# First attention of a decoder kernel: queries projected with features on the partitions, for two batches at a time

## The chip, the cores and the metric

The kernel runs on one core of a Trainium2 chip. The core has a matrix engine (TensorE), three engines for vectors (VectorE, ScalarE, GpSimd), a queue that issues DMAs (SyncE, SP in the rows), an on-chip memory of 128 partitions (SBUF) and eight accumulation banks of 128 x 512 fp32 (PSUM), which GpSimd cannot reach in this kernel. The metric is the device time of one execution in microseconds (us), lower is better; the time of before is the median of three.

## The reference

Two decoder layers over x of 4 batches x 256 tokens x 256 features, each of attention, an adjacency or bilinear step with a side input, and a feed-forward step. The change concerns the first attention alone: 32 heads, queries from a low rank of 192, keys and values from a latent of 64 and a shared rotary part of 64.

```python
q = rms_norm(hidden_states @ q_a_w, q_a_ln_w) @ q_b_w
q = q.reshape(B, S, NH, DQK)
q_pass, q_rot = (q[..., :DN], q[..., DN:])
ckv = hidden_states @ kv_a_w
c_kv, k_rot = (ckv[..., :KVLR], ckv[..., KVLR:])
kv = rms_norm(c_kv, kv_a_ln_w) @ kv_b_w
...
q_rot = apply_rope(q_rot, pos)      # x1*cos - x2*sin, x1*sin + x2*cos on halves of 32
k_rot = apply_rope(k_rot[:, :, None, :], pos)[:, :, 0, :]
scores = (einsum('bqhd,bkhd->bhqk', q_pass, k_pass) + einsum('bqhd,bkd->bhqk', q_rot, k_rot)) * scale
scores = jnp.where(causal[None, None], scores, jnp.finfo(scores.dtype).min)
p = jax.nn.softmax(scores, axis=-1)
out = jnp.einsum('bhqk,bkhd->bqhd', p, v).reshape(B, S, NH * DV)
return out @ o_w
```

Beside it, independent of it and needed right after it, stands an adjacency per batch: similarities of the side input, of which the top 76 of 256 in each row are kept, through a sigmoid, and mixed with the normalised attention output.

## The kernel before, in words

The key part of kv_b is absorbed into the query's weights, so that every head has a query of 128 features for each token: 64 latent ones and 64 rotary ones. All heads share the keys of a batch (`keyT`, features on the partitions), and the values are the latent part of `key_tok`. The 32 heads are worked in 8 groups `g` of 4. Products of projections are made of fp32 numbers split in a high and a low part, three products for each; a query bank is five products of 512 columns.

For each batch `b` and group `g` the steps are: `q` (TensorE: two banks, one for each tile of 128 tokens, tokens on the partitions, 4 heads x 128 features in the columns; VectorE: three multiplications into `rope_buf`; ScalarE: latent part to `q_tok`; GpSimd: adds the two rotary products into `q_tok`), `qT` (TensorE: 8 transposes of 128 x 128 back into the same banks; ScalarE: two copies to `qT`), twice `s` (scores of two heads; VectorE masks and takes the row extremes in two pieces, 256 and 128 wide, since the causal half is left out; ScalarE: exp), `norm` (VectorE reciprocal, GpSimd multiplies), `pT` (transposes of probabilities), then `pv`, `out`. A group's weights come by DMA into one of two raw buffers and are split into high and low parts (`w_q`, `w_v`).

The adjacency's steps are `adj_sim` (TensorE), ten rounds `adj_top` on VectorE (MAX of 8, MATCH_REPLACE), two masks `adj_mask` on VectorE and `adj_T`; batch `b` starts after the masks of `b - 1`. Behind the attention of a batch stand statistics, normalisation and mixing (`att_stats`, `att_mix`, `mix_norm`), and then the router and the experts.

What sets the order is a planner, which runs when the program is built: every step has parts with an engine and a cost, needs, and places that it holds (banks, `probs`, `qT`, `rope`, `q_tok`). It takes the step that can start soonest on an engine, among near ones the one with the longest way to the end, and writes an order for each engine. Each engine then executes its own list strictly in that order, and waits on semaphores. A change of steps or costs thus moves instructions on all engines. `mm` is line 1011 (every product), `transpose` 1025, ScalarE's `copy` 1389, VectorE's `tt` 1680, GpSimd's `tt` 2136.

## Time and profile before

| | |
|---|---|
| median of three runs | 800.99 us (800.61 to 803.52) |
| the profiled execution | 801.79 us |
| its span in the trace | 799.9 us, 15236 instructions |
| mean granted TensorE clock | 0.976 |
| busy: TensorE, its weight loads, VectorE, ScalarE, GpSimd | 751.4 (94%), 636.4 (80%), 566.4 (71%), 506.4 (63%), 354.6 (44%) us |
| chain that ended last | TensorE 85%, VectorE 11% |

Engines in the rows: PE is TensorE, PEld its weight loads, DVE VectorE, ACT ScalarE, POOL GpSimd, SPq the queue of SyncE. Busy shares are averages over stages with different bounds; which engine sets the time in a stage is read from the chain of waits there. A product's listed duration overlaps the next one, so its price in a dense row is the distance between starts. fp32 products that aren't split by hand appear as two instructions each.

### The profile page before, as it was taken

Reading aid. Unit: us, or ns where it says so; the run is one execution under the profiler, and the core shown is the slowest. Engines: PE = TensorE matmul, PEld = TensorE weight load, DVE = VectorE, ACT = ScalarE, POOL = GpSimd, SP = SyncE. Lnnn points to the kernel's source line nnn. Section 1 sums busy time; section 2 is a strip of 40 time slices with the busy share of each in tenths; the row PEclk is TensorE's granted clock in tenths of the full one; section 3 lists DMA queues with packets and bytes.
Section 4 is the critical chain, followed back from the end, with each engine's and each line's share of the span. In section 5 each row is a group of like instructions: output and inputs, shape, how many; then the busy total and the mean of one; then the engine's idle time right before and its main releaser. Section 6 shows DMA issues by size and latency. Waiting matters only on the chain.

```text
span 799.9 us, 15236 instructions
## 1 busy us (share of the span) xinstructions
PE 751.4 (94%) x5060; PEld 636.4 (80%) x5060; DVE 566.4 (71%) x1909; ACT 506.4 (63%) x1321; POOL 354.6 (44%) x595
## 2 busy tenths in 40 slices
PE   6899999999999999999987999999879999969995
PEld 4578888888888888888765887888768888748884
DVE  2879889888679854656897756546787575656844
ACT  2669683878558774786654646676457757626541
POOL 1436441554236441566662445544752122347640
PEclk9899999999999999999997999999999999979998
DMA  8700002200040001100020021111110001000320
GB/s 274 208 3 2 2 2 74 74 1 2 1 146 2 2 1 40 41 2 1 1 80 0 1 77 38 45 40 40 40 42 3 2 3 31 13 2 0 119 66 27
DMA packets 27479, 30.95 MB, mean 39 GB/s; under 512 B 4412, under 2 KB 24518, under 8 KB 27400
## 3 DMA queue, kind: packets, MB, share of 16 engines
q1 hardware_dynamic: 27400, 29.96, 12.1%
q8 instruction: 41, 0.67, 0.4%
q14 instruction: 38, 0.31, 0.1%
HBM read 28.77 MB, written 1.05 MB: 37 GB/s over the span
## 4 chain that ended last, share of the span: by engine, by line
PE 85%; DVE 11%; issue 1%; POOL 1%; DMA 1%; ACT 1%; SPq 0%; DVEq 0%; ACTq 0%
PE bank L1011 73%; PE bank L1025 12%; DVE x L1677 1%; DVE y L1683 1%; POOL probs L2133 1%; DVE bn L1711 1%; DMA xT_plain<-in_xT 1%; DVE probs L1828 1%; DVE top_tok L2044 1%; DVE rope_tmp L1680 1%; DVE g_pair_lo L1680 0%; DVE key_tok L1683 0%; DVE u_pair_lo L1680 0%; DVE stat L1683 0%; DVE router_buf L1683 0%
## 5 line engine op out<-in xcount | busy, mean ns | idle before, releaser
L2133 POOL TENSOR_SCALAR probs<-probs,soft 128x256 f32<-128x256 f32 (+1 forms) x256 | 104.9, 431 | 76.2 <-DVE soft L1836 75.9
L1475 ACT ACTIVATE probs<-probs,soft 128x256 f32<-128x256 f32 (+1 forms) x256 | 113.0, 447 | 2.0 <-DVE soft L1828 2.0
L2136 POOL TENSOR_TENSOR w_split_lo<-w_raw,w_split_hi 128x512 fp32r<-128x512 f32 (+2 forms) x57 | 74.3, 1312 | 65.3 <-ACT w_split_hi L1389 65.2
L2136 POOL TENSOR_TENSOR q_tok<-rope_buf 128x256 f32<-128x256 f32 x64 | 47.7, 748 | 106.1 <-DVE rope_buf L1680 105.9
L1011 PE MATMUL bank<-keyT,qT 128*128 128x256 f32 (+1 forms) x512 | 92.3, 328 | 0.0
L1011 PEld LDWEIGHTS bank<-keyT,qT 128*128 128x128 f32 x512 | 82.9, 190 | 9.4 <-issue 0.3
L1828 DVE CUSTOM_DVE_ANT_0 probs<-bank,mask 128x256 f32<-128x256 f32 (+1 forms) x256 | 78.5, 354 | 9.4 <-PE bank L1011 9.0
L1680 DVE TENSOR_TENSOR rope_buf<-bank,rope 128x128 f32<-128x128 f32 (+1 forms) x192 | 52.0, 328 | 32.6 <-PE bank L1011 32.2
L1389 ACT ACTIVATE qT<-bank 128x512 f32<-128x512 f32 (+1 forms) x96 | 53.6, 592 | 23.3 <-PE bank L1025 22.8
L1011 PE MATMUL bank<-w_split_hi,xT_hi 128*128 128x512 f32 (+1 forms) x160 | 64.8, 405 | 2.1 <-DVE xT_lo L1683 1.6
L1389 ACT ACTIVATE probsT<-bank 128x384 f32<-128x384 f32 x128 | 54.0, 489 | 13.4 <-PE bank L1025 13.3
L1011 PE MATMUL bank<-w_split_hi,xT_lo 128*128 128x512 f32 (+1 forms) x160 | 61.9, 387 | 0.0
L2136 POOL TENSOR_TENSOR probs<-probs 128x512 f32<-128x512 f32 x32 | 41.6, 1309 | 39.2 <-ACT probs L1558 38.1
L1011 PE MATMUL bank<-w_split_hi,g_pair_hi 128*128 128x256 f32 x192 | 54.6, 284 | 2.7 <-issue 1.5
L1011 PE MATMUL bank<-w_split_lo,g_pair_hi 128*128 128x256 f32 x192 | 54.0, 281 | 0.0
L1011 PE MATMUL bank<-w_split_hi,g_pair_lo 128*128 128x256 f32 x192 | 54.0, 281 | 0.0
L1389 ACT ACTIVATE q_tok<-bank 128x256 f32<-128x256 f32 x64 | 24.2, 385 | 46.6 <-DVE rope_buf L1680 46.2
L1011 PE MATMUL bank<-xT_hi,w_split_hi 128*128 128x512 f32 x128 | 52.1, 407 | 0.0
L1025 PE MATMUL bank<-identity,probs 128*128 128x128 f32 x384 | 50.7, 274 | 1.1 <-POOL probs L2133 1.0
L1011 PE MATMUL bank<-xT_hi,w_split_lo 128*128 128x512 f32 x128 | 51.4, 401 | 0.0
L1011 PE MATMUL bank<-xT_lo,w_split_hi 128*128 128x512 f32 x128 | 51.3, 401 | 0.0
L2044 DVE TENSOR_REDUCE top_tok<-bank 128x2 f32<-128x512 f32 x64 | 40.3, 686 | 14.2 <-PE bank L1011 13.8
(227 smaller groups left out, 2077.1 us busy)
## 6 DMA issues: line engine op xcount, KB each, us to landing
w_raw<-in_w_o SPq DMA_DIRECT2D x8, 512.0 KB, 4.7
w_raw<-in_w_nopeT SPq DMA_DIRECT2D x8, 384.0 KB, 3.1
w_raw<-in_w_gateT SPq DMA_DIRECT2D x8, 256.0 KB, 2.7
w_raw<-in_w_upT SPq DMA_DIRECT2D x8, 256.0 KB, 3.1
w_raw<-in_w_downT SPq DMA_DIRECT2D x8, 256.0 KB, 3.6
w_raw<-in_L_ffn_Wup SPq DMA_DIRECT2D x7, 256.0 KB, 2.8
w_raw<-in_L_ffn_Wgate SPq DMA_DIRECT2D x7, 256.0 KB, 3.1
w_raw<-in_L_ffn_Wdown SPq DMA_DIRECT2D x7, 256.0 KB, 3.7
```

Source lines behind the costliest of these rows:

```text
L1011: return t.matmul(out, lhsT, rhs, start=start, stop=stop, skip_group_check=shared)
L1025: return t.transpose(out, in_, ident[0:rows, 0:rows])
L1389: return s.activation(out, in_, ACT.Copy, **kw)
L1475: ins = s.activation(p[:, at], p[:, at], ACT.Exp, bias=st[:, 0, r:r + 1], scale=-1.0, accum_out=st[:, 1, r:r + 1])
L1677: return v.tensor_scalar(out, in0, s1, s2, op0, op1)
L1680: return v.tensor_tensor(out, in0, in1, op)
L1683: return v.scalar_tensor_tensor(out=out, in0=in0, scalar=s, in1=in1, op0=op0, op1=op1)
L1711: own(v.bn_stats(bn[place][:, i, 0:6], tile))
L1828: v.tensor_tensor_reduce(out=p[:, at], in0=bank_of(("s", b, g, h))[:, at], in1=mask, scale=-SCALE0, scalar=3.0e38, op0=ALU.add, op1=ALU.mi ...
L2044: v.reduce_max(top_tok[top1_turns.place[b, g]][:, :, 2 * p + j], two(bank_of(("s1", b, h))), AX).then_inc(top1.sem, 1)
L2133: return g_.tensor_scalar(out, in0, s1, s2, op0, op1)
L2136: return g_.tensor_tensor(out, in0, in1, op)
```

## The change

- A query step is now `("q", n, g, p)`: a half `n` of the batch (two batches, 512 tokens), a group and a pair `p` of its heads. The weights are the fixed operand and the normalised low-rank queries the moving one, so features come out on the partitions. There are two banks, "rot" and "lat", each with two heads of 64 features, and no transposes. Banks of weights are stored by kind; the rotary weights of each pair of heads are swapped on the host.
- Rotary step: VectorE multiplies the rot bank with a sine table and with a cosine table (`rope0_T`, features on the partitions, 128x512 each). Four DMAs move the sine product by 32 partitions into `qT`, so that the halves are swapped. GpSimd adds the cosine product, in two additions of 64 partitions. ScalarE copies the latent bank with two copies of 64 partitions (`q_lat`).
- For an odd head latent and rotary features stand in exchanged halves of the partitions, so there is a second `keyT` with its halves exchanged, made by two DMAs for each half of the batch (`key_swap`).
- `qT` has 4 buffers of 2 heads x 512 tokens (it had 3 of 4 heads x 256), `rope` 3 (2 of them in the space of the plain `xT`), `q_tok` is gone; some temporaries moved into `probs`. The planner has new costs for these steps. GpSimd waits for the completion of the previous step before and after each `q`.
- The scores of an odd batch are placed behind those of the even batch before it.

```diff
-            stage(("q", b, g), "PE 2.4, DVE 1.7, ACT 0.9, POOL 1.5", ("w_q", g), ("down_T", 0), ("down_T", 1), ("zero",),
...
-            stage(("qT", b, g), "PE 0.87, ACT 1.1", ("q", b, g), items=2)
+        stage(("key_swap", h), "SP 1.2, DMA 0.8, WAY 2", By(("down_T", h), "ACT"))
+                stage(q, "PE 2.35, DVE 1.4, SP 2.2, DMA 0.8, WAY 2, POOL 2.7", ("w_q", g), ("down_T", 0), ("down_T", 1), ("zero",),
...
+                stage(("q_lat", n, g, p), "ACT 1.2", By(q, "PE"))
+    SWAPS = [(at + i * DR // 2, at + (1 - i) * DR // 2) for at in (0, DR) for i in range(2)]
+    def turned_rows(j):
+        return (slice(KVLR, P), slice(0, KVLR)) if j == 0 else (slice(0, DR), slice(DR, P))
... TensorE
-                for i, tile in enumerate(batch_tiles(b)):
-                    out = wait_bank(("q", b, g, i))[:, :]
-                    at = slice(tile * P, (tile + 1) * P)
-                    mm3(out, qaT[:, 0, at], w_q[:, 0, :, :], True, False)
-                    mm(out, qaT.hi[:, 1, at], w_q.hi[:, 1, :, :], False, False)
-                    mm(out, qaT.lo[:, 1, at], w_q.hi[:, 1, :, :], False, True).then_inc(q_ready.sem, 1)
-            elif name == "qT":
...
+                for kind in (1, 0):
+                    out = wait_bank(("q", n, g, p, ("lat", "rot")[kind]))[:, :]
+                    first, rest = (w_q[:, c, kind, 2 * p:2 * p + 2, :] for c in range(2))
+                    mm3(out, first, qaT[:, 0, at], True, False)
+                    mm(out, rest.hi, qaT.hi[:, 1, at], False, False)
+                    mm(out, rest.hi, qaT.lo[:, 1, at], False, True).then_inc(q_ready.sem, 1)
... scores
+                    at, keys_b = b % 2 * S, keyT[j][:, cols(b)]
+                    mm(out[:, 0:S], q[:, j, at + P:at + S], keys_b)
+                    mm(out[:, S:S + P], q[:, j, at:at + P], keys_b[:, 0:P]).then_inc(scored.sem, 1)
... ScalarE
+                for j in range(2):
+                    rows = turned_rows(j)[1]
+                    ins = copy(dst[rows, j, :], src[rows, :])
... VectorE
-                    tt(rp[:, 0, :, :], rot, cos, ALU.mult)
-                    tt(rp[:, 1, :, 0:hd], rot[:, :, hd:DR], sin_lo, ALU.mult)
-                    tt(rp[:, 1, :, hd:DR], rot[:, :, 0:hd], sin_hi, ALU.mult).then_inc(rope_parts.sem, 1)
+                for kind, done in ((1, rope_sin), (0, rope_cos)):
+                    tt(rp[:, kind, :].rearrange("p (b s) -> p b s", s=S), src,
+                       rope0_T[:, kind, :].unsqueeze(1).to_broadcast([P, HALF // S, S]), ALU.mult).then_inc(done.sem, 1)
... GpSimd
+            if before is not None and "q" in (name, before[0]):
+                w.wait_ge(*done(before))
...
+                w.wait_ge(*rope_cos[n, g, p])
+                w.wait_ge(*q_swapped(n, g, p))
+                for j in range(2):
+                    rows = turned_rows(j)[0]
+                    ins = tt(dst[rows, j, :], dst[rows, j, :], rp[rows, 0, :], ALU.add)
... SyncE
+                w.wait_ge(*rope_sin[n, g, p])
...
+                for src, dst in SWAPS:
+                    j = 0 if src >= KVLR else 1
+                    q.dma_start(qT[place][dst:dst + DR // 2, j, :],
+                                rope_buf[rope_turns.place[n, g, p]][src:src + DR // 2, 1, :]).then_inc(q_swapped_at[place], 16)
```

How the order moves. TensorE at the first queries of the first group (xT_hi and xT_lo hold the normalised low-rank queries, w_split the weights), before:

```order
L1011 MATMUL bank0<-w_split0_hi,xT_hi 128x512
L1011 MATMUL bank0<-w_split0_hi,xT_lo 128x512
L1011 MATMUL bank6<-ctxT,w_qk_x 64x512
L1011 MATMUL bank5<-ctxT,w_qk_x 64x512
L1011 MATMUL bank7<-w_kv_x,ctxT 128x64 x8
L1025 MATMUL bank1<-identity,q_tok0 128x128 x4
L1025 MATMUL bank0<-identity,q_tok1 128x128 x4
L1011 MATMUL bank3<-qk_x 128x256
L1011 MATMUL bank2<-qk_x 128x256
L1011 MATMUL bank0<-w_split0_hi,xT_hi 128x512
L1011 MATMUL bank0<-w_split0_lo,xT_hi 128x512
```

and now:

```order
L1042 MATMUL bank3<-xT_lo,w_split0_hi 128x512
L1042 MATMUL bank2<-ctxT,w_qk_x 64x512
L1042 MATMUL bank4<-ctxT,w_qk_x 64x512
L1042 MATMUL bank6<-w_kv_x,ctxT 128x64 x8
L1042 MATMUL bank1<-xT_hi,w_split0_hi 128x512
L1042 MATMUL bank1<-xT_lo,w_split0_hi 128x512
L1042 MATMUL bank1<-xT_hi,w_split0_lo 128x512
L1042 MATMUL bank1<-xT_hi,w_split0_hi 128x512
L1042 MATMUL bank1<-xT_lo,w_split0_hi 128x512
L1042 MATMUL bank5<-xT_hi,w_split0_hi 128x512
L1042 MATMUL bank5<-xT_lo,w_split0_hi 128x512
```

Before, the transposes of the first batch's queries stand behind two banks of projections and some products of the side input. Now six banks of projections (thirty products, the last of them in the first row) stand there, no transposes follow, and two more pairs of banks come before the first score.

SyncE's queue behind the constants (keyT and qT rows are the new moves inside SBUF, w_raw the next groups' weights), before:

```order
L2290 DMA w_raw0<-in_w_v_latT 128x256
L2291 DMA w_raw0<-in_w_o 128x1024
L2285 DMA w_raw1<-in_w_nopeT 128x768
L2286 DMA w_raw1<-in_w_k_latT 128x256
L2287 DMA w_raw1<-in_w_rot 128x256
L2289 DMA w_raw1<-in_w_rot 64x256 x2
L2290 DMA w_raw1<-in_w_v_latT 128x256
```

and now:

```order
L2388 DMA keyT1<-keyT0 64x512
L2389 DMA keyT1<-keyT0 64x512
L2398 DMA qT0<-xT_plain 32x512 x4
L2398 DMA qT1<-xT_plain 32x512 x4
L2398 DMA qT2<-rope_buf2 32x512 x4
L2318 DMA w_raw1<-in_w_nopeT 128x768
L2319 DMA w_raw1<-in_w_k_latT 128x256
L2320 DMA w_raw1<-in_w_rot 128x256
L2322 DMA w_raw1<-in_w_rot 64x256 x2
L2323 DMA w_raw1<-in_w_v_latT 128x256
L2324 DMA w_raw1<-in_w_o 128x1024
L2398 DMA qT3<-xT_plain 32x512 x4
```

The swaps of the first three query steps stand between the loads of two groups, and that of the fourth waits behind a load.

VectorE at the end of the first attention, behind its last softmax step (ctx_pair and y with a bank are steps of the heads' output, bn and stat the statistics of a batch, sim, best and adjacency the adjacency), before:

```order
L1836 RECIPROCAL soft1<-soft1 128x2
L1680 TENSOR_TENSOR ctx_pair1_lo<-bank5,ctx_pair1_hi 128x512
L1680 TENSOR_TENSOR y<-bank2,y 128x512
L1677 TENSOR_SCALAR x<-y,bn4,stat4 128x256 x2
L1680 TENSOR_TENSOR ctx_pair0_lo<-bank0,ctx_pair0_hi 128x512
L1680 TENSOR_TENSOR y<-bank7,y 128x512
L1677 TENSOR_SCALAR x<-y,bn0,stat0 128x256 x2
L1680 TENSOR_TENSOR y<-bank5,y 128x512
L1711 BN_STATS bn1<-y 128x6 x2
L1714 BN_AGGR bn1<-bn1 128x2 x2
L1676 TENSOR_SCALAR stat1<-bn1 128x2
```

and now:

```order
L1698 TENSOR_TENSOR ctx_pair1_lo<-bank1,ctx_pair1_hi 128x512
L1698 TENSOR_TENSOR y<-bank3,y 128x512
L1698 TENSOR_TENSOR y<-bank0,y 128x512
L1694 TENSOR_SCALAR sim0<-sim0 128x256
L1892 RECIPROCAL sim0<-sim0 128x256
L1701 SCALAR_TENSOR_TENSOR adjacency<-sim0,best0 128x256
L1698 TENSOR_TENSOR y<-bank6,y 128x512
L1694 TENSOR_SCALAR sim1<-sim1 128x256
L1892 RECIPROCAL sim1<-sim1 128x256
L1701 SCALAR_TENSOR_TENSOR adjacency<-sim1,best1 128x256
L1729 BN_STATS bn1<-y 128x6 x2
L1732 BN_AGGR bn1<-bn1 128x2 x2
```

The masks of the last adjacency (sim0 and sim1), which stood some 300 instructions earlier, now stand among the last outputs and ahead of the statistics of the last batches.

## Rows read from the trace of the kernel before

**Rows 1.** Windows: engines' busy us (count), clock, DMA share, GB/s
```profile
42.00:378.00 336.00, 335.33 (x2408) 290.46 (x2408) 258.89 (x1129) 240.16 (x788) 151.83 (x312) 1.00 0.08 23
...
400.00:420.00 20.00, 16.94 (x97) 13.85 (x92) 18.19 (x55) 10.52 (x16) 12.09 (x24) 0.91 0.25 80
```

**Rows 2.** Chain of waits, 42 to 380 us: start, us, what
```profile
by line: PE bank L1011 77.8%; PE bank L1025 19.8%; POOL probs L2133 0.7%; DVE probs L1828 0.6%; issue 0.5%; ACT qT L1389 0.4%; DVE rope_buf L1680 0.1%; DVE soft L1828 0.1%; DVE soft L1836 0.0%; ACTq L120 0.0%
...
52.02 0.61 ACT qT L1389
...
72.53 1.31 PE bank L1011 x8
...
90.50 3.65 PE bank L1011 x18
...
98.08 0.87 PE bank L1025 x8
```

**Rows 3.** Groups of the query steps: busy us, mean ns, idle before
```profile
L1680 DVE TENSOR_TENSOR rope_buf<-bank,rope 128x128 f32<-128x128 f32 x128 | 30.6, 281 | 0.0
...
L1680 DVE TENSOR_TENSOR rope_buf<-bank,rope 128x256 f32<-128x256 f32 x64 | 27.0, 423 | 32.6 <-PE bank L1011 32.2
...
L1389 ACT ACTIVATE qT<-bank 128x512 f32<-128x512 f32 x64 | 34.7, 593 | 17.6 <-PE bank L1025 17.3
...
L1389 ACT ACTIVATE q_tok<-bank 128x256 f32<-128x256 f32 x64 | 24.2, 385 | 46.6 <-DVE rope_buf L1680 46.2
...
L2136 POOL TENSOR_TENSOR q_tok<-rope_buf 128x256 f32<-128x256 f32 x64 | 47.7, 748 | 106.1 <-DVE rope_buf L1680 105.9
```

**Rows 4.** Groups with shapes near the new instructions'
```profile
L1389 ACT ACTIVATE qT<-bank 64x512 fp32r<-64x512 f32 x32 | 18.9, 590 | 5.7 <-PE bank L1025 5.4
...
L1680 DVE TENSOR_TENSOR y<-bank,x 128x512 f32<-128x512 f32 x16 | 10.8, 689 | 9.2 <-PE bank L1011 9.2
...
L1680 DVE TENSOR_TENSOR rope_tmp<-bank,rope 128x512 f32<-128x512 f32 x8 | 7.6, 953 | 2.1 <-PE bank L1011 2.1
...
L2136 POOL TENSOR_TENSOR probs<-probs 128x512 f32<-128x512 f32 x32 | 41.6, 1309 | 39.2 <-ACT probs L1558 38.1
```

**Rows 5.** DMAs: ns of one issue; KB and us to landing
```profile
L2358 SPq DMA_DIRECT2D qT<-topT x64: 558/558/676, 592.1 to 692.0; - x64
...
out<-x SPq DMA_DIRECT2D x4, 256.0 KB, 2.6
...
w_raw<-in_w_o SPq DMA_DIRECT2D x8, 512.0 KB, 4.7
```

**Rows 6.** Timeline of VectorE at the stage's end
```profile
387.74 0.55 DVE L1836 RECIPROCAL soft<-soft 128x2 f32<-128x2 f32 x6
...
396.37 0.69 DVE L1680 TENSOR_TENSOR ctx_pair_lo<-bank,ctx_pair_hi 128x512 fp32r<-128x512 f32 x1 [0.99 <-ACT ctx_pair_hi L1389]
...
404.80 0.75 DVE L1711 BATCH_NORM_STATS2 bn<-y 128x6 f32<-128x256 f32 x2
...
413.75 1.28 DVE L1680 TENSOR_TENSOR u_pair_lo<-probs,u_pair_hi 128x512 fp32r<-128x512 f32 x2
```

**Rows 7.** VectorE on the adjacency: two groups, and one mask's timeline
```profile
L1865 DVE MAX8 best<-sim 128x8 f32<-128x256 f32 x80 | 29.8, 412 | 0.7 <-ACT sim L1389 0.6
...
L1869 DVE MATCH_REPLACE8 sim<-best,sim 128x256 f32<-128x256 f32 x72 | 28.9, 409 | 0.0
...
138.83 1.75 DVE L1878 RECIPROCAL sim<-sim 128x256 f32<-128x256 f32 x1
...
140.62 0.48 DVE L1683 SCALAR_TENSOR_TENSOR adjacency<-sim,best 128x256 f32<-128x256 f32 x1
```

**Rows 8.** Timeline at the router, GpSimd beside VectorE
```profile
417.54 2.69 POOL L2136 TENSOR_TENSOR probs<-probs 128x512 f32<-128x512 f32 x2 [1.23 <-ACT probs L1558]
...
417.56 1.27 DVE L1683 SCALAR_TENSOR_TENSOR router_buf<-iota,rt_stat,router_buf 128x8 f32<-128x8 f32 x1
...
422.77 0.23 DVE L1683 SCALAR_TENSOR_TENSOR router_buf<-iota,rt_stat,router_buf 128x8 f32<-128x8 f32 x1
```

More of the change, by code:

```diff
@@ L287, in unit_readers @@
     if n < U_EXPERT:
-        return [[("q", b, n) for b in range(B)], [("q", b, n) for b in range(B)], [("out", b, n) for b in range(B)]]
+        queries = [("q", h, n, p) for h in range(NHALF) for p in range(GH // 2)]
+        return [queries, queries, [("out", b, n) for b in range(B)]]
     if n < U_QKV:
@@ L758, in write_program @@
     vo_lo = signal("vo_lo", keys("w_v"))
-    rope_parts = signal("rope_parts", keys("q", range(TB)))
+    rope_sin = signal("rope_sin", keys("q"))
+    rope_cos = signal("rope_cos", keys("q"))
     top = signal("top", [k + (r,) for k in heads(keys, "s") for r in range(2)])
@@ L796, in write_program @@
     rot_lo = signal("rot_lo", keys("w_q"))
-    q_rot = signal("q_rot", keys("q", range(TB)))
+    q_rot = signal("q_rot", keys("q"))
     normed = signal("normed", heads(keys, "norm"))
@@ L828, in top_landed, with q_swapped, qT_free @@
         return top_landed_at[place], 16 * 2 * HEADS_PER_TILE * (rank + 1)
+    def q_swapped(n, g, p):
+        place = qT_turns.place[n, g, p]
+        rank = [k for k in keys_in_order_of("SP")("q") if qT_turns.place[k] == place].index((n, g, p))
+        return q_swapped_at[place], 16 * len(SWAPS) * (rank + 1)
+    def qT_free(n, g, p):
+        before = qT_turns.before[n, g, p]
+        if before is None:
+            return []
+        n, g, p = before
+        return [latest(scored, [(b, g, 2 * p + j) for b in halves(n) for j in range(2)])]
     UNIT_LOADS = [(5, 2)] * NG + [(3, 0)] * NE + [(1, 0)] + [(3, 0)] * NU
@@ L977, in xT_room @@
         if tag == "experts":
-            return [latest(q_ready, [(b, g, TB - 1) for g in range(NG)])]
+            return [latest(q_ready, [(b // 2, g, p, "lat") for g in range(NG) for p in range(GH // 2)])]
         if tag == "attn1":
```

186 lines of the change are left out of this document (95 added, 91 removed).

## The prediction, made before the changed kernel was run

> **What bounds the kernel now.** I read the row of the stretch first, then the chain of waits in it, then the groups of instructions, and last the timeline at the stage's end. The first attention runs from about 42 to about 390 us. In [rows 1] TensorE is busy for 335.33 of the 336 us from 42 to 378, at a granted clock of 1.00, while VectorE has 258.89, ScalarE 240.16 and GpSimd 151.83. The chain in that stretch says the same [rows 2]: 77.8% products and 19.8% transposes of TensorE, a little over 2% of anything else, among it two waits of 0.6 us for a copied query. So here a microsecond of TensorE work is a microsecond of time, as long as the other engines still feed it in the new order. After 380 this changes: VectorE is busy 18.19 of the 20 us from 400 to 420 and TensorE only 16.94 [rows 1]. From the last softmax step (its reciprocals start at 387.74) to the first split of an expert's operand (413.75) VectorE stands still for only about 3 us, the longest wait being 0.99 us [rows 6]. The end of the stage therefore has another bound than its body, and the change must be costed in each.
>
> **TensorE, the term that counts.** Eight transposes of queries for each of 32 pairs of batch and head group go away. In the chain one such set stands as 0.87 us between products that start when it ends [rows 2], so 109 ns for each. 256 x 0.109 = 27.9 us. The projection keeps its number: before, 64 banks of five products with 512 columns, now 32 steps of two banks of five with 512 columns, with operands in swapped roles. The scores keep their shapes too. TensorE gets no new work: -27.9 us.
>
> **ScalarE.** Gone: 64 copies of 128x512 to qT (34.7 us) and 64 of latent parts (24.2 us) [rows 3]. New: 64 copies of 64 partitions x 512. A copy of 64x512 takes 590 ns, as much as one with 128 partitions (593) [rows 3, 4]: 37.8 us. ScalarE is relieved by 21.1 us; it was not on the chain, so 0.
>
> **VectorE.** Gone: 64 multiplications of 128x256 and 128 of 128x128 (27.0 + 30.6 us) [rows 3]. New: 64 of 128x512 out of a bank. The nearest row with the same shape and a plain second operand takes 689 ns, the one with a rotary table in 16-wide pieces 953 ns [rows 4]: 44 to 61 us. I take 44, since the new table is read in runs of 256. That is -13.5 us, bounds -13.5 to +3.4, under TensorE's cover in the body: 0.
>
> **GpSimd.** Gone: 64 additions at 748 ns, 47.7 us [rows 3]. New: 64 additions of 64 partitions x 512. No row shows 64 partitions on this engine; 128x512 takes 1309 ns [rows 4], half of it would be 0.65. I take 1.31, because for ScalarE half the partitions were no cheaper: 83.8 us, +36.1. With 151.83 us before, that makes 188 us of a stretch of 308: 61%. These additions stand in the same queue as the normalisations of the probabilities, and from now on each waits for a DMA; behind a late one stand the normalisations, then the transposes of probabilities, then the products with the values. New completion waits around each step add an empty moment each on this engine, hidden the same way.
>
> Beside that, a rule of the Trainium skill (GPSIMD Engine Reference, section 2.1): each of the eight cores goes to the next instruction as soon as its own 16 partitions are done. The two additions of a step use opposite halves, so by that page a pair might take about 1.3 us and not 2.6, and GpSimd would gain nothing and lose nothing; no row of before shows two such additions. The changed trace would show it as pairs that take as long as one addition.
>
> **The new way of a query.** SP issues four DMAs for each of 32 steps, at 558 ns (the row of the small DMAs to qT) [rows 5]: 2.2 us, 71 us in all on a queue that mostly waits for free weight buffers. The landing of 64 KB between two places in SBUF is not shown. 256 KB to memory land in 2.6 us, and the last part of a group's weights in 4.7 us [rows 5]; I take 3, and up to 4.7 where a weight load of the next group is ahead, as in SyncE's order, where a load stands among the first swaps. The way from the rotary bank to a usable query is then 0.7 + 2.2 + 3 + 2.6 = 8.5 us, up to 10.2, where it was 0.98 (three VectorE instructions), 0.75 (GpSimd), 0.87 (transposes) and 0.6 us (copy) [rows 2, 3]: 3.2 us. What hides it: the order places three projections (30 products, 7 us at 0.234 us for one: a piece of the chain with ten products and the scores of two heads has 3.65 us, the scores alone 1.31 [rows 2]) and the context products ahead of the first score, and four query buffers, each for two batches and two heads, let a score run behind its projection by up to sixteen head-and-batch products. The same shape recurs where a new group starts. Where the cover is just too short, TensorE waits. Bounds: 0, and 8 group starts x 1.7 us (10.2 less 8.5) = 14 us. The waits that the old order has there are of 0.61 us [rows 2]; I take four of these, one for each pair of groups that the planner runs together: +2.4 us.
>
> **The start.** The larger table (256 KB) joins the constants that the keys' rotary step waits for. Half of the 512 KB that land in 4.7 us [rows 5] would be 2.4 us; the bounds are 0 and 2.4. I take 0, since it comes behind the first weights and ahead of a megabyte of x, none of which the first projections wait for.
>
> **The end of the stage, where something comes back.** In the old order the top-k rounds and masks of the fourth batch's adjacency are done when 168 of 256 softmax operations have passed. In the new one they fall to the very end: behind the last softmax operation stand, in addition, four MAX (1.65 us), two MATCH_REPLACE (0.8), two masks of a reciprocal and a product (2 x (1.75 + 0.48) = 4.5) and a subtraction each, priced like a MATCH_REPLACE (0.8) [rows 7], three additions out of a bank (2.1 at 689 ns) [rows 4] and one block of statistics (0.75) [rows 6], less four small reciprocals (0.4) [rows 6]. Sum 10.1 us. VectorE was full there, so they are not free; one of its waits, 0.99 us [rows 6], can take some in: +9.1 us. From the last softmax to the expert's split this gives 26.0 + 9.1 = 35 us. Bounds: 0 (VectorE, relieved before, arrives early and fills waits for TensorE) and 10.
>
> **Sum.** Span 799.9 - 27.9 + 2.4 + 9.1 = 783.5 us. The profiled run took 801.79, 1.9 more than its span, and is 0.8 above the median of the three (800.99): 783.5 + 1.9 - 0.8 = 784.6, which I call 784. Behind the first attention the order of TensorE is the old one up to a few products, so all of it stays.
>
> **Rivals.**
> - A, nothing comes back: the adjacency's tail fits into waits of VectorE, and no query is late. 801 - 28 = 773. For it: VectorE has 77 us of room in 336. Against it: that room lies earlier, and the old tail is almost without a wait.
> - B, group starts are exposed: 14 us instead of 2.4. 784.6 + 11.6 = 796. For it: the way of a query grows from 3.2 to 8.5 us and a weight load can stand in front of a swap. Contention belongs here: a VectorE product on 128x8 elements took 1.27 us while GpSimd did two additions of 128x512, and 0.23 us without them [rows 8], and the change adds 36 us of such additions. The Trainium skill (GPSIMD Engine Reference, section 1) says the same, that GpSimd's SBUF port is shared with VectorE instructions that read two inputs from SBUF; the trace agrees. In the body few VectorE instructions have two such inputs.
> - C, slower: GpSimd's queue becomes the bound. It stops in order at each of 32 query steps for a swap that hasn't landed, with normalisations behind it. If each stop costs TensorE x us, the time is 782 + 32x; it passes 801 at x = 0.6. With the growth of the additions wholly exposed (36.1 us over 32, x = 1.1) it is 817. For it: in-order queue, and 61% load with DMA waits inside. Against it: GpSimd waited 106 us for the rotary parts in the old kernel [rows 3] and TensorE stood still for none of it, and eight buffers of probabilities allow a normalisation to be late.
> - D, the transposes weren't on the path, so the removal gives nothing: 799 to 803. Against it stands the whole of [rows 2].
>
> **Chances.** Forecast 0.55 (its own range 779 to 789), A 0.17, B 0.20, C 0.05, D 0.03. Differences below 0.5% (4 us) can't be told from none with this kernel. Faster: the first three, 0.92. Same: D and a little of C, 0.04. Slower: C, 0.04. The range 772 to 797 takes in A and B and leaves out 0.1 to 0.2.
>
> **What would show it.** In the changed profile: TensorE still busy in nearly all of the stretch from 42 to about 350, with 256 instructions fewer; the query additions of GpSimd at 1.3 us; swaps landing in about 3 us; GpSimd's waits for a DMA short, and TensorE's waits behind them under 3 us in sum; between the last softmax and the expert's split some 35 us of VectorE with the two masks in it. I am wrong if TensorE shows waits for ScalarE's or GpSimd's query parts of more than 5 us in sum, if the last softmax step comes later than 366 us, or if the gain shrinks in a stage behind the first attention.

## The result, and the profile after

The changed kernel takes 780.0 us (median of 4 executions, 778.93 to 782.45) against 800.9 us before (4, 800.61 to 803.52): ratio 0.9736, 95% interval 0.9705 to 0.9767, 21 us. Two more comparisons gave 0.9764 (0.9721 to 0.9807) and 0.9729 (0.9698 to 0.9759). The forecast was 784 in a range of 772 to 797.

The windows of the first attention after the change answer to [rows 1]. Columns: stretch, its length, busy time and count of TensorE, its weight loads, VectorE, ScalarE and GpSimd, granted clock, DMA share, GB/s.

```profile
42.00:350.00 308.00, 307.62 (x2177) 262.91 (x2176) 241.76 (x1011) 226.87 (x745) 190.03 (x322) 1.00 0.21 55
350.00:370.00 20.00, 17.71 (x150) 15.26 (x146) 19.31 (x59) 10.66 (x31) 12.54 (x30) 1.00 0.00 1
370.00:390.00 20.00, 12.66 (x54) 10.74 (x55) 19.18 (x49) 3.81 (x7) 7.75 (x18) 0.66 0.25 79
```

TensorE is as full as before, in a first attention whose scores take 33.5 us less (table below); GpSimd has risen from 151.83 us of 336 to 190.03 of 308. In the tail VectorE is full, TensorE is not, and the granted clock is 0.66 on average in a stretch in which TensorE was busy for 12.66 us of the 20.

The groups of the query steps, which answer to [rows 3] (columns: line, engine, operation, names, shapes, count, busy us, mean ns, idle before):

```profile
L2150 POOL TENSOR_TENSOR qT<-qT,xT_plain 64x512 f32<-64x512 f32 x44 | 56.6, 1285 | 49.8 <-DMA qT<-xT_plain 47.7
...
L1416 ACT ACTIVATE qT<-bank 64x512 f32<-64x512 f32 x64 | 37.9, 592 | 41.3 <-PE bank L1042 40.8
...
L1698 DVE TENSOR_TENSOR xT_plain<-bank,rope_T 128x512 f32<-128x512 f32 x44 | 28.3, 686 | 10.3 <-PE bank L1042 10.1
...
L2150 POOL TENSOR_TENSOR qT<-qT,rope_buf 64x512 f32<-64x512 f32 x20 | 25.8, 1288 | 15.2 <-DMA qT<-rope_buf 14.1
```

The rotary buffers live partly in the place of xT, so the trace calls them xT_plain and rope_buf. GpSimd's 64 additions take 56.6 + 25.8 = 82.4 us (83.8 were worked out), and a pair on opposite halves of the partitions takes 2.60 us. GpSimd stands for 61.8 us before them, for a swap that hasn't landed. The swaps themselves, from the page of DMAs (size, median us to landing) and from the view of their tile (ns of one issue: min/median/max):

```profile
qT<-xT_plain SPq DMA_DIRECT2D x88, 64.0 KB, 2.0
```
```profile
L2398 SPq DMA_DIRECT2D qT<-xT_plain x88: 507/591/1527, 35.4 to 337.5; - x88
```

Who TensorE waited for from 350 to 420 us (us in all, times, longest). From 36 to 350 it waited for 0.3 us in all, and never for a query part.

```profile
PE bank L1056 <- DVE adjacency L1701: 5.5, 1, 5.5
PE bank L1042 <- DVE xT_lo L1698: 4.3, 2, 3.7
PE bank L1042 <- DVE u_pair_lo L1698: 2.1, 1, 2.1
PE bank L1056 <- DVE x L1695: 1.8, 1, 1.8
PE bank L1042 <- DVE ctx_pair_lo L1698: 1.6, 2, 1.4
```

**Where the time went.** Three marks cut every profile: the first and the last start of a score product, and the last start of a router product that closes the tail. The view of a tile gives them as "first to last"; before, then after:

```profile
L1011 PE MATMUL bank<-keyT,qT x512: 271/326/483, 46.8 to 386.3; 128*128 128x128 f32 x86, 128*128 128x256 f32 x85
...
L1011 PE MATMUL bank<-w_router_hi,xT_hi x16: 167/253/376, 406.7 to 439.2; 128*128 128x8 f32 x16
```
```profile
L1042 PE MATMUL bank<-keyT,qT x512: 272/326/483, 46.5 to 352.7; 128*128 128x128 f32 x86, 128*128 128x256 f32 x85
...
L1042 PE MATMUL bank<-w_router_hi,xT_hi x16: 168/253/354, 380.4 to 412.8; 128*128 128x8 f32 x16
```

The same marks in each profile (both kernels were profiled again, unchanged, in the experiments below):

| us | start to first score | body: first to last score | tail: to last router product | rest | span |
|---|---|---|---|---|---|
| before, 2 profiles | 46.8, 44.1 | 339.5, 339.6 | 52.9, 53.0 | 360.7, 363.9 | 799.9, 800.6 |
| after, 3 profiles | 46.5, 50.0, 48.1 | 306.2, 306.0, 305.9 | 60.1, 61.2, 62.1 | 364.3, 364.9, 364.3 | 777.1, 782.1, 780.4 |
| difference of means | +2.7 | -33.5 | +8.2 | +2.2 | -20.4 |

The body repeats within 0.3 us, so a microsecond can be read there that the whole kernel hides in its spread. Start and body belong together: the first score comes 14.6 to 16.1 us behind the first projection, before 10.8 and 12.3. That is the order's doing: 40 projection products stand ahead of it (30, and ten of one more pair of banks; the text on the change says two more pairs, the trace shows one) where 20 and eight transposes stood, products that the body has no more. It is not the length of the query's way as executed: in the same order without swaps and additions the distance is 14.8 us, with the swaps doubled 16.0 (both kernels below). From the first projection to the last score product it is 351.75 and 350.4 us before, 320.8, 322.1 and 322.0 after: -29.5. Where these 29.5 us stood can be summed from the starts in the trace, each product being given the time to the next one's start: the 256 transposes of queries fill 29.7 us in both profiles of before (116 ns each), the score products 85.2 before and 85.1 after, the projections 78.8 and 77.4 before, 78.0, 79.4 and 79.5 after. So the transposes are the whole of it, and the swapped roles of the projection's operands cost nothing that shows.

### The profile page after: what moved, and what is told of

It reads as the page before. It is cut to its first block, busy times and chain, and to the rows that moved or that the text cites. A ratio compares the mean times of both kernels' runs of the same rounds, so it can differ in the third digit from the quotient of the medians.

```text
span 777.1 us, 14587 instructions
## 1 busy us (share of the span) xinstructions
PE 720.7 (93%) x4804; PEld 608.5 (78%) x4804; DVE 556.9 (72%) x1781; ACT 489.3 (63%) x1257; POOL 389.2 (50%) x595
## 4 chain that ended last, share of the span: by engine, by line
PE 80%; DVE 10%; issue 4%; SPq 2%; POOL 2%; ACT 1%; DMA 1%; DVEq 0%; POOLq 0%; ACTq 0%
PE bank L1042 70%; PE bank L1056 9%; DVE x L1695 2%; DVE bn L1729 1%; SPq L2398 1%; DVE y L1701 1%; DVE y L1698 1%; POOL probs L2147 1%; DVE top_tok L2058 1%; DMA qT<-xT_plain 1%; DVE rope_tmp L1698 1%; DVE sim L1892 0%; DVE g_pair_lo L1698 0%; DVE bn L1732 0%; DVE probs L1842 0%
## 5 line engine op out<-in xcount | busy, mean ns | idle before, releaser
L2147 POOL TENSOR_SCALAR probs<-probs,soft 128x256 f32<-128x256 f32 (+1 forms) x256 | 104.8, 431 | 55.4 <-DVE soft L1850 54.0
L1042 PE MATMUL bank<-xT_hi,w_split_hi 128*128 128x512 f32 x256 | 105.3, 411 | 1.5 <-DVE xT_lo L1701 1.5
L1042 PE MATMUL bank<-xT_lo,w_split_hi 128*128 128x512 f32 x256 | 102.0, 398 | 0.0
L1416 ACT ACTIVATE qT<-bank 64x512 f32<-64x512 f32 (+1 forms) x96 | 56.8, 591 | 48.0 <-PE bank L1042 40.8
L1042 PEld LDWEIGHTS bank<-keyT,qT 128*128 128x128 f32 x512 | 80.2, 191 | 7.7 <-issue 0.7
L2150 POOL TENSOR_TENSOR qT<-qT,xT_plain 64x512 f32<-64x512 f32 x44 | 56.6, 1285 | 49.8 <-DMA qT<-xT_plain 47.7
L1042 PE MATMUL bank<-xT_hi,w_split_lo 128*128 128x512 f32 x192 | 76.6, 399 | 0.0
L2150 POOL TENSOR_TENSOR probs<-probs 128x512 f32<-128x512 f32 x32 | 41.6, 1309 | 40.7 <-ACT probs L1576 39.9
L1042 PEld LDWEIGHTS bank<-xT_hi,w_split_hi 128*128 128x128 f32 x256 | 49.3, 193 | 14.9 <-issue 5.4
L1416 ACT ACTIVATE probsT<-bank 128x384 f32<-128x384 f32 x128 | 52.9, 494 | 8.8 <-PE bank L1056 8.6
L1042 PEld LDWEIGHTS bank<-xT_lo,w_split_hi 128*128 128x128 f32 x256 | 49.4, 193 | 9.3
L2058 DVE TENSOR_REDUCE top_tok<-bank 128x2 f32<-128x512 f32 x64 | 40.3, 686 | 15.7 <-PE bank L1042 15.3
L1042 PE MATMUL bank<-probsT,key_tok 128*64 128x256 f32 (+1 forms) x512 | 50.2, 335 | 0.0
L1493 ACT ACTIVATION_READ_ACCUMULATOR probs<-probs,soft 128x1 f32 x256 | 49.2, 192 | 0.0
```

What stands on the lines that cost most here:

```text
L1042: return t.matmul(out, lhsT, rhs, start=start, stop=stop, skip_group_check=shared)
L1416: return s.activation(out, in_, ACT.Copy, **kw)
L1493: ins = s.activation(p[:, at], p[:, at], ACT.Exp, bias=st[:, 0, r:r + 1], scale=-1.0, accum_out=st[:, 1, r:r + 1])
L2058: v.reduce_max(top_tok[top1_turns.place[b, g]][:, :, 2 * p + j], two(bank_of(("s1", b, h))), AX).then_inc(top1.sem, 1)
L2147: return g_.tensor_scalar(out, in0, s1, s2, op0, op1)
L2150: return g_.tensor_tensor(out, in0, in1, op)
```

## Experiments

Edits are shown as short diffs; `...` is what is left out. Times are medians, and ratios are to the kernel before, run on the same chip in the same comparison (its median 800.0 us beside the first four, 800.7 beside the next four, 801.2 beside the last four).

### Both kernels again

> The kernel before, unchanged, profiled once more. Question: the changed kernel began its first projection 2.6 us earlier (31.93 us against 34.55 us in the profiled executions), although nothing in front of it was meant to get faster. If that is the spread of one execution, this profile should put the start of the first projection anywhere between 31.5 and 35 us, and off 34.55 by 0.5 us or more. If it belongs to the change, it should be at 34.5 within 0.3 us again.

> The changed kernel, unchanged, profiled and timed once more. By the reading that the change is worth 21 us: 780 us, ratio 0.971 to 0.977. First projection: if its early start (31.93 us) is chance, it moves by 0.5 us or more; if it belongs to the change, 31.9 within 0.3. Behind the router the clock fell to 0.56 to 0.64 in stretches in which it was 0.67 to 1.00 before, at a cost of 2.3 us: if chance, these stretches differ in this profile.

> The changed kernel once more, unchanged, beside the other three on one chip: 780 to 784 us, ratio 0.974 to 0.978; the first projection anywhere from 31.5 to 34 us, the last score product 320.8 to 322.1 us behind it, the first pair of the experts 36 to 37 us behind that, and 388 to 390 us from there to the end.

Measured: before 802.4 us in one execution, after 783.4 us (4 executions) and 780.2 us (6). The first projection starts at 34.55 and 33.28 us before, at 31.93, 33.87 and 31.96 after, and at 31.54 in a kernel below that has the start of before: the early start in the first profile of after is no property of the change. Nor is the slow stretch behind the experts: 66 products took 11.64 us in the first profile of after, 9.63 in the second, and 9.63 before. The clock near the start is as unsteady: in every one of these profiles some 4 us between 24 and 48 us are granted 0.71 or less, at another place each time, with an early first projection or a late one. The third run of after came out within its ranges (322.0 us from the first projection to the last score product, 36.8 to the first pair of the experts, 389.6 from there to the end), but for the ratio, 0.9729 where 0.974 to 0.978 was expected.

### The transposes given back to TensorE alone

```diff
                     out = wait_bank(("q", n, g, p, ("lat", "rot")[kind]))[:, :]
+                    for i in range(4):
+                        transpose(out[:, i * P:(i + 1) * P], ident[:, :])
```

> The changed kernel with 256 transposes of 128x128 given back to TensorE (four of the identity into each bank just before a projection is written over them); the transposed values are used by nobody, no other engine gets work. Theory (TensorE is full in the first attention, so each of its instructions is paid for): 256 x 109 ns = 27.9 us, less up to 5.5 us that the tail no longer waits for the last adjacency, since VectorE has more time before it: 780 + 22 to 28 = 802 to 808 us. Rival (the transposes themselves were covered, and the gain came from the copies and waits that went with them): 780 to 788 us.

Measured: 807.9 us (805.2 to 809.1), ratio 1.0075 (1.0037 to 1.0113), 24.5 to 27.7 us above the changed kernel. From the first projection to the last score product 345.9 us, +24.3: 95 ns for each transpose (91 by the sum of starts). The group, in a by-shape view from 30 to 410 us:

```profile
L1056 PE MATMUL bank<-identity 128*128 128x128 f32 x256 | 39.0, 275 | 0.7 <-DVE xT_lo L1703 0.7
```

The mean of 275 ns is the whole way of one through the pipeline; 39.0 us is the union of overlapping ones, and neither is the price. The tail stayed at 61.4 us with 5.5 us of waiting for the adjacency, though VectorE had 24 us more. So the transposes are the gain, and rival D has fallen, as has the rival put here (780 to 788 us). That more time for VectorE would shorten the tail was wrong: the adjacency's place in the order stayed, and so did the wait.

### The kernel before without most of its transposes

```diff
-                    for h in range(GH):
-                        ins = transpose(bank_of(("q", b, g, i))[:, h * P:(h + 1) * P], src[:, h, :])
+                    h = GH - 1
+                    ins = transpose(bank_of(("q", b, g, i))[:, h * P:(h + 1) * P], src[:, h, :])
```

> The kernel before with three of every four transposes of the queries left out (192 of 256), all else and the order as it was; the part of the computation that is left out is the transposing of the queries of three heads in four. Theory (the gain is TensorE's alone, and what came back in the tail came from the new order, which puts the last adjacency behind the last softmax): 192 x 109 ns = 20.9 us, nothing comes back: 780 us, with less than 27.5 us between the last softmax and the first pair of the experts (26.0 before). Rival (whatever shortens the body brings VectorE's tail out): the distance grows by 5 us or more, 785 us and more.

Measured: 787.2 us (783.2 to 788.3), ratio 0.9801 (0.9752 to 0.9851): 12.8 us for 192 transposes. By its time this lies in the rival's range (785 and more) and not at the theory's 780; by the distance, which tells the two apart, the theory holds: from the last score product to the first pair of the experts 27.4 us, exactly as before, where the rival wanted 5 us more. Body 322.7 us, -16.9 (88 ns for each transpose); tail 51.0, nothing comes back. From the first projection to the last score product it is 338.5 us, -12.6 (66 ns): some of the missing microseconds lie ahead of the body, where first projection and first score are 15.8 us apart (12.3 and 10.8 before), at a low clock; another 4 are missing in the body, and behind the router this profile takes 365.5 us for 360.7 and 363.9. These two windows are of this kernel; before has 1.00 in both:

```profile
40.00:44.00 4.00, 4.00 (x15) 2.73 (x14) 1.13 (x5) 2.69 (x6) 0.00 (x0) 0.60 0.01 3
44.00:48.00 4.00, 4.00 (x12) 3.15 (x11) 1.28 (x5) 0.38 (x1) 0.73 (x1) 0.54 0.00 0
```

A body shortened by 17 us without a new order costs nothing in the tail. The rival's mechanism, by which any shorter body brings VectorE's tail out, is refuted as far as this shortening goes; where the 8 us between 12.8 and 20.9 went is described and not explained.

### The last adjacency at other places

```diff
-        stage(("adj_T", b), "PE 0.45, DVE 0.7", ("adj_mask", b, 0), ("adj_mask", b, 1), ("load", "identity"),
+        stage(("adj_T", b), "PE 0.45, DVE 0.7", ("adj_mask", b, 0), ("adj_mask", b, 1), ("load", "identity"), ahead=16 if b == 3 else 0.0,
```

> The changed kernel with the last batch's adjacency started earlier in the order (one number of the planner, 16 us of urgency for that batch alone; same instructions). Theory (the order puts the last masks behind the last softmax, TensorE then waits 5.5 to 6.2 us for the adjacency, and VectorE has room before that): the distance from the last score product to the first pair of the experts falls from 36 to 37 us to 28 to 31 us, TensorE's wait for the adjacency goes, and the time falls by 4 to 7 us, to 776 to 779 us against the 783.4 us that the changed kernel gave in the last comparison. Rival (VectorE's work in the tail is due to the shorter body, wherever it stands in the order): the distance stays within 2 us or the body becomes longer by as much, and the time is the same within 2 us.

The same with `ahead=8`:

> The changed kernel with the last batch's adjacency moved half as far as in the earlier trial (last masks behind 232 and 240 of 256 softmax rows; 208 and 212 there, 256 in the changed kernel). There the wait for the adjacency went, but the body became 2 us longer and the experts' first products waited elsewhere, with no gain. Theory (VectorE is full from the last softmax to the experts, so its order only chooses what TensorE waits for): within 2 us of the changed kernel, 781 to 785 us. Rival (a better place exists between the two): 777 to 780 us.

And in the kernel before, the other way:

```diff
-              *[("adj_mask", b - 1, i) for i in range(TB) if b],
+              *[("adj_mask", b - 1, i) for i in range(TB) if b], *[("s", 0, 6, 0)] if b == 3 else [],
```

> The kernel before with the last batch's adjacency held back by one more dependency in the planner, so that its last masks stand behind 240 and 256 of the 256 softmax rows on VectorE (164 and 168 before; 256 in the changed kernel). No instruction is added or taken. Theory (that place in the order is what the tail of the changed kernel pays for): the distance from the last score product to the first pair of the experts grows from 27.4 us to 32 to 37 us, and the time by 4 to 9 us, to 804 to 809 us. Rival (the tail grew because the body became shorter): distance 27.4 within 1 us, 800 us.

Measured:

| | time, us | ratio (95%) | body | tail | both | last score to first pair |
|---|---|---|---|---|---|---|
| after, 3 profiles | 780.0, 783.4, 780.2 | 0.9736, 0.9764, 0.9729 | 306.0 | 61.1 | 366.3, 367.2, 368.0 | 36.1, 36.9, 36.8 |
| earlier (16) | 783.9 | 0.9793 (0.9777 to 0.9810) | 308.6 | 60.2 | 368.8 | 31.2 |
| a little earlier (8) | 783.1 | 0.9776 (0.9744 to 0.9807) | 315.3 | 52.6 | 367.9 | 29.6 |
| before | | | 339.6 | 53.0 | 392.4, 392.6 | 27.4, 27.4 |
| before, late | 804.5 | 1.0033 (1.0007 to 1.0058) | 339.4 | 54.7 | 394.1 | 29.8 |

How that distance is filled, before and after (windows from the last score product to the first pair of the experts; busy times in the order given above):

```profile
386.30:413.70 27.40, 25.22 (x179) 21.06 (x177) 23.75 (x77) 14.85 (x38) 18.02 (x43) 0.94 0.18 58
```
```profile
352.70:388.80 36.10, 26.46 (x178) 22.55 (x177) 34.69 (x98) 11.66 (x28) 16.85 (x41) 0.81 0.14 44
```

VectorE's busy time grows by 10.9 us, and it stands still for 1.4 us where it stood for 3.7. Its adjacency work there, by its groups in that stretch: none before, 3.5 us in the late variant of before, 9.1 us after (two reciprocals of 1754 ns, four MAX, two MATCH_REPLACE, four masking instructions and two additions). The distance follows it with the right sign, +2.4 and +9 us, but the late variant of before stayed under its forecast of 32 to 37 us, since only the last of its masks really fell behind the last score product; that its time of 804.5 us lies within the forecast 804 to 809 proves little, since body and tail together grew by 1.6 us only. In the changed kernel, the earlier place does remove TensorE's wait of 5.5 us, and nothing is won. What TensorE waited for from 350 to 420 us there:

```profile
PE bank L1042 <- DVE xT_lo L1698: 6.2, 2, 3.2
PE bank L1056 <- DVE x L1695: 3.0, 1, 3.0
PE bank L1042 <- DVE u_pair_lo L1698: 2.1, 1, 2.1
PE bank L1056 <- POOL probs L2147: 1.2, 2, 0.9
```

The wait for the adjacency has turned into longer waits for the normalised x (3.0 us for 1.8), its split (6.2 for 4.3) and GpSimd's probabilities (1.2 for none), and the body is 2.6 us longer. The body then also has a wait of 1.0 us for a query part, which the changed kernel never has. With the milder edit the sum is the same again, with 5.2 us of waits for GpSimd's probabilities, and its time of 783.1 is within the 781 to 785 expected. For the earlier place my forecast of 4 to 7 us gained was wrong, and the rival as I put it only half right: the distance did shrink, but body and tail together stayed at 366 to 369. Neither place beats the changed kernel. Whether some other order gets the 8 us back stays open.

### How much room the query's way has

Without swaps and additions (ScalarE copies all 128 partitions in the same number of instructions, and SyncE's loop over the swaps is empty; the queries' rotary half is left out):

```diff
-                w.wait_ge(*q_swapped(n, g, p))
-                for j in range(2):
-                    rows = turned_rows(j)[0]
-                    ins = tt(dst[rows, j, :], dst[rows, j, :], rp[rows, 0, :], ALU.add)
-                ins.then_inc(q_rot.sem, 1)
+                tt(rp[:, 0, 0:2], rp[:, 0, 0:2], rp[:, 0, 0:2], ALU.add).then_inc(q_rot.sem, 1)
...
-                    ins = copy(dst[rows, j, :], src[rows, :])
+                    ins = copy(dst[:, j, :], src[:, :])
```

> The changed kernel without the swap transfers and without GpSimd's additions: ScalarE copies all 128 partitions of each latent bank, so the queries' rotary half is left out of the computation. VectorE's multiplications stay, the order stays. Theory (the way costs TensorE nothing): 783 us within 2 us of the changed kernel. Rival (some of the 21 us gained would have been 25 without it, in the waits of the softmax for GpSimd, say): 776 to 780 us.

With the additions twice, and with one of the two twice (the second diff line is then under `if j == 0`):

```diff
                     rows = turned_rows(j)[0]
+                    tt(rp[rows, 1, :], rp[rows, 0, :], rp[rows, 1, :], ALU.add)
                     ins = tt(dst[rows, j, :], dst[rows, j, :], rp[rows, 0, :], ALU.add)
```

> The changed kernel with each of GpSimd's 64 query additions done twice (the extra one into the rotary buffer, read by nobody): 64 x 1.285 = 82 us more of GpSimd, which was busy 190 us of the 308 us of the first attention and would be busy 272 of them. Theory (GpSimd has room, and its waits were for transfers): 783 to 790 us, TensorE's waits for POOL probs grow to a few us. Rival (the queue of GpSimd is next to bound): each extra microsecond shows, 800 us or more. If the Trainium skill's page on GpSimd (GPSIMD Engine Reference, section 2.1: cores move on when their own 16 partitions are done) held for these additions, two on opposite halves of the partitions would overlap and cost half; every pair seen so far took 2.6 us.

> The changed kernel with one of the two additions of each query part done twice: 32 x 1.29 = 41 us more of GpSimd, 3.9 us per part in place of 2.6 (5.2 with both twice, which cost 47 us). Theory of the burst (the parts of two head groups come as a bunch of eight, four times; GpSimd loses 8 x 1.3 = 10.3 us on TensorE in each bunch, and with 20.6 us lost per bunch the price was 12 us, so some 9 us of each bunch are covered): 4 x 1 to 2 us, 787 to 792 us. Rival (a price in proportion, 0.57 us for each microsecond of GpSimd): 41 x 0.57 = 23 us, 803 to 809 us. Rival (busy share: GpSimd would be busy 231 of 308 us, so it has room): 783 us within 2.

With the swaps twice, one set behind the other:

```diff
-                for src, dst in SWAPS:
+                sem, all_landed = q_swapped(n, g, p)
+                for i, (src, dst) in enumerate(SWAPS + SWAPS):
+                    if i == len(SWAPS):
+                        w.wait_ge(sem, all_landed - 16 * len(SWAPS))
```

> The changed kernel with the way of every query part lengthened: SyncE waits until the four swap transfers have landed and issues the same four again, which GpSimd's addition then waits for. Some 4 us more of way (2.2 to 2.4 of issue, 2.0 of landing) for each of 32 parts, 130 us more of SyncE's queue. Theory (a query part is ready early enough, its way has slack): 783 us within 4 us, TensorE's waits for query parts under 4 us in all. Rival (the way is used up, group starts are exposed): 32 x 4 us would be 128 us if every part were late, 8 group starts x 4 us = 32 us if only those were: 800 us or more.

Measured (GpSimd's busy time and the clock are from 42:350, which holds a smaller part of the work where the body is longer; the waits are TensorE's, 36 to 440 us, for query parts and probabilities of GpSimd):

| | time, us | ratio (95%) | body | GpSimd busy of 308 | waits for GpSimd | granted clock |
|---|---|---|---|---|---|---|
| no swaps, no additions | 778.7 | 0.9714 (0.9693 to 0.9735) | 305.1 | 114.7 | 0 | 0.99 |
| changed kernel | 780 to 783 | 0.973 to 0.976 | 306.0 | 188.5 | 0.3 | 1.00 |
| one addition twice | 796.9 | 0.9934 (0.9906 to 0.9962) | 323.4 | 210.4 | 10.2 | 0.98 |
| both twice | 831.0 | 1.0365 (1.0345 to 1.0385) | 359.5 | 219.7 | 35.6 | 0.95 |
| swaps twice | 862.6 | 1.0760 (1.0735 to 1.0785) | 389.8 | 142.9 | 55.4 | 0.91 |

The whole way costs the body 0.9 us. The time is 1.3 to 4.7 us below the changed kernel's and lies in the rival's range (776 to 780) and not in the theory's (781 to 785); but the body and the waits, where the rival's mechanism would have to stand, show 0.9 and 0.3 us, and the rest is in start and tail, where kernels differ by that much between executions. So the theory is right about the way, within about a microsecond.

The other three forecasts, all of which said that there is room, were wrong: 796.9 us for 787 to 792, 831.0 for 783 to 790, 862.6 for 779 to 787. The way has next to no room. GpSimd's share of 61% said there was plenty, and 41 us more of additions already cost 17 in the body (the profiled execution, 800.9 us, is the slowest of ten, which begin at 789.1; by the medians it is 14 to 17), where busy share said 0 to 2, my theory of bunches 4 to 8, and proportion 23. SyncE's longer way is dearer still, at a GpSimd that is busy for 143 us of 308.

TensorE's waits for GpSimd with one addition twice, with both twice and with the swaps twice (us in all, times, longest). Most of it is for the query parts themselves, rival B's mechanism; the rest is for normalised probabilities that stand behind them in GpSimd's queue, rival C's:

```profile
PE bank L1042 <- POOL qT L2150: 7.7, 6, 2.3
PE bank L1056 <- POOL probs L2147: 2.5, 8, 0.6
```
```profile
PE bank L1042 <- POOL qT L2150: 25.3, 13, 3.5
PE bank L1056 <- POOL probs L2147: 10.3, 8, 3.0
```
```profile
PE bank L1042 <- POOL qT L2150: 36.6, 13, 5.0
PE bank L1056 <- POOL probs L2147: 18.8, 7, 6.4
```

Two things in the traces go with it. First, the query parts come in bunches of four. In the changed kernel the rotary products of one bunch start at 115.0, 119.5, 123.5 and 127.2 us, some 4 us apart. GpSimd's two additions need 2.6 us of that; with one of them twice 3.9 us, with both twice 5.2, and with the swaps twice the parts come out of SyncE's queue 6.4 us apart (GpSimd's additions then start at 151.6, 158.0, 164.4 and 170.8). The way of the four parts, from the rotary product's start to the end of the last addition, is 8.6, 7.3, 7.3 and 7.4 us in the changed kernel, 11.3, 12.0, 13.2 and 14.6 with both additions twice, and 12.7, 14.6, 17.0 and 19.0 with the swaps twice: each part falls further behind. With one addition twice it is 10.3, 9.9, 9.8 and 10.0, so GpSimd keeps pace there, and this bunch alone doesn't explain the 17 us. GpSimd with both additions twice, inside such a bunch:

```profile
144.44 1.26 POOL L2150 TENSOR_TENSOR qT<-qT,xT_plain 64x512 f32<-64x512 f32 x1
145.78 1.28 POOL L2150 TENSOR_TENSOR xT_plain<-xT_plain 64x512 f32<-64x512 f32 x1
147.02 1.27 POOL L2150 TENSOR_TENSOR qT<-qT,xT_plain 64x512 f32<-64x512 f32 x1
148.35 1.35 POOL L2150 TENSOR_TENSOR xT_plain<-xT_plain 64x512 f32<-64x512 f32 x1
149.66 1.26 POOL L2150 TENSOR_TENSOR qT<-qT,xT_plain 64x512 f32<-64x512 f32 x1
```

It adds without a gap, and TensorE stands waiting at the head of the scores. TensorE's timeline and the windows around that wait:

```profile
150.97 5.49 PE L1042 MATMUL bank<-keyT,qT 128*128 128x256 f32 x16 [3.28 <-POOL qT L2150]
```
```profile
146.00:150.00 4.00, 1.70 (x11) 1.40 (x9) 3.88 (x14) 1.90 (x9) 3.94 (x4) 0.99 0.00 0
150.00:154.00 4.00, 3.03 (x9) 2.67 (x10) 1.41 (x11) 2.70 (x12) 3.86 (x4) 0.50 0.00 0
154.00:158.00 4.00, 4.00 (x18) 2.77 (x18) 2.01 (x14) 3.07 (x14) 3.44 (x5) 0.66 0.00 0
```

Second, the wait is paid again: behind the stretch in which TensorE was busy for 1.70 of 4 us its granted clock is 0.50, then 0.66, that is the lower of its two levels, 1.2 GHz, for most of 8 us. An estimate from these traces: waits plus the clock's loss (the body times one less its mean clock, 0.989, 0.953 and 0.912 over the three bodies) give 10.2 + 4 = 14, 35.6 + 17 = 53 and 55.4 + 34 = 90 us, against bodies longer by 17.4, 53.5 and 83.8. The two parts overlap where the clock is low while TensorE waits, so they needn't add up exactly. Body by wait, a microsecond of such waiting costs 1.5 to 1.7.

## Why the prediction was right, and where it was not

The time, the sign and the mechanism came out: 780.0 against 784. By its own steps:

- **What bounds the kernel**: right. In the body TensorE's work is the time, before and after, and the tail has another bound. The transposes given back alone bring the gain back (24.5 us and more), so rival D is out. Of the signs of being wrong, none came: 0.3 us of waits for GpSimd, last softmax step at 358.4 us, and what the later stages lost is within the spread (last point).
- **TensorE, -27.9 us (109 ns for each transpose)**: measured -29.5 us from the first projection to the last score product, 115 ns for each. The sum of starts in the old kernel gives 116 ns, so 109, read from one row, was 6% low. Given back as identities they cost 95 ns; 192 of them taken from the kernel before gave 88 ns in the body and 66 from the first projection on. What an exact price would be depends on what stands beside them, and why the last one is so low isn't shown.
- **Waits at group starts, +2.4 us (bounds 0 and 14)**: they were 0. No score waited for a query part. The way itself was sized well: from the rotary product's start to the end of the second addition 7.3 to 10.6 us, 8.3 in the mean (first profile), for 8.5 to 10.2 (swap issue 591 ns for 558, landing 2.0 us in the median for 3, and 4.3 for the fourth part's, behind a weight load, for 4.7; additions 2.6 us a pair as taken). What was mis-sized is the cover: ahead of the first score stand 40 projection products and not 30. Rival B's mechanism exists, as the doubled swaps and additions show, but this kernel stays just short of it.
- **ScalarE and VectorE at 0**: right; 592 and 686 ns for 590 and 689. The optimistic end for VectorE held (the bound was 953); that this is due to the long runs in which the rotary table is read was my reason, and no run tests it.
- **GpSimd, +36.1 us, hidden**: the busy time was right (82.4 us for 83.8), and its cost was nil (0.9 us of body with the whole way gone). But that it would be hidden was not worked out: a share of 61% and waits of 106 us in the old kernel stood for it, and in the runs above a share of 68% had lost 17 us. Right, then, with some luck. The Trainium skill (GPSIMD Engine Reference, section 2.1) has each core start the next instruction as soon as it has finished its own 16 partitions; the trace doesn't agree: two additions on opposite halves of the partitions show no overlap here, in the pairs of 2.60 us and in the rows above, where an addition on the other half starts 1.2 to 1.3 us behind the last. With that overlap four additions would take as long as two take now, and doubling them would have cost nothing.
- **Rival C**: given 0.05 with x from 0.6 as the point at which it decides. It did not happen, but the runs put it near: one more addition in each step cost 17 us, 0.5 us a step.
- **The start at 0**: not told apart. The first projection starts anywhere from 31.5 to 34.6 us in the profiles of these two kernels and of the one with the start of before.
- **The tail, +9.1 us**: from the last score product to the first pair of the experts +9.2 us (27.4 to 36.6 on average); to the last router product +8.2. The terms: 10.1 us of work less one wait of 1.0; measured 10.9 us of work (23.75 to 34.69) less 2.2 us of waits taken in, in the first profile, so both are near. That the adjacency instructions there also sum to 9.1 us is chance. That it is a debt of the order alone was my reading in the expectations, and it half fell: placed earlier, the instructions leave the tail, and the sum of body and tail stays. TensorE's waits from 350 to 420 us sum to 15.3 us, where they were 10.5 from 380 to 446 before, so 4.8 more; the rest of the 8.2 goes with a lower clock over the whole tail (0.83, 0.83 and 0.78 in the three profiles, 0.87 in both of before), which is a reading and not tested.
- **The rest at 0**: +2.2 us in the mean, from two profiles of before that differ by 3.2 themselves; nothing to explain with.

The forecast's sum of 783.5 for the span was made of -27.9 + 2.4 + 9.1; measured it is -29.5, 0 and +8.2, with -1.3 for the start (33.9 to 32.6 in the mean) and +2.2 for the rest, both within the spread: -20.4, which gives a span of 779.9.

## What to carry over

Where one engine is full, price an instruction that leaves it by the spacing of its starts in the chain, and cost each end of the stage by itself: the engine that is full there may take part of the gain back (here 8.2 of 29.5 us). A work item that moves to a side engine is hidden by what waits between its bunches, not by that engine's busy share; compare its rate with the producer's in the bunch, and expect a microsecond of waiting that gets through to cost more than itself, since the clock falls behind it (in these runs 1.5 to 1.7 us). And a wait that an edit of the order removes has gained nothing until the sum of the stretch around it is smaller.

## What the runs showed of the hardware

- On GpSimd an addition over 64 of 128 partitions (64x512) takes as long (1285 ns) as one over all (128x512, 1309 ns), and one on the other half doesn't start beside it. ScalarE's copy of 512 columns is the same with 64 partitions (592 ns, after) and with 128 (593 ns, before).
- A 64 KB transfer between two places in SBUF lands 2.0 us after issue (median of 128, at most 4.5), hardly sooner than 256 KB on their way to memory (2.2 in the same profile). Issuing takes 0.59 us each, so for a swap in four pieces the issue (2.4 us) is longer than the landing.
- TensorE's granted clock fell to 0.50 behind a stretch of 4 us in which it was busy for 1.70. With the swaps twice, where many such places follow one another, the mean clock of the body was 0.91.
